# Reordering one iteration of a fused two-convolution kernel on TensorE, with small sums moved to another PSUM bank

## What is computed

```python
# stage 1, on g = groupnorm(x)
out = conv3x3(sign(tile(g, 4)), sign(w1), groups=4)           # 256 channels
out = relu(batchnorm(out))
out = conv3x3(sign(out), sign(w2), groups=4)
out = sum over the 4 groups of batchnorm(out) * lambda
x = x + relu(out + g)
# stage 2, on g = groupnorm(x)
mid = g * resized_mask                                         # one mask per image
att = sigmoid(conv7x7([mean_c(mid), max_c(mid), mask]))
out = mid * att
x = x + relu(5 * (instancenorm(out) * gamma + beta))
```

## Time and profile before

| | |
|---|---|
| median of 3 runs | 230.12 us (230.0 to 231.04) |
| profiled execution | 229.95 us, span of its instructions 228.1 us |
| granted TensorE clock, mean | 0.976 of full speed |
| TensorE matmul busy | 199.2 us (87%) |
| VectorE, ScalarE, GpSimd busy | 167.2 (73%), 174.7 (77%), 154.8 us (68%) |
| iteration 5 (no attention) | 9.94 us |
| iterations 13 and 14 | 23.25 us |
| from the loop's last turn to the end | 34.57 us |

### The profile page before, as it was taken

One profiled execution on the slowest core, in us unless ns is written; L12 is line 12 of the kernel. 1 busy time (PEld: TensorE's weight loads), 2 busy tenths in 40 slices (PEclk: granted clock), 3 DMA queues, 4 the chain that ended last, 5 costly groups with the idle time before them and its releaser, 6 DMA issues.

```text
span 228.1 us, 8994 instructions
## 1 busy us (share of the span) xinstructions
PE 199.2 (87%) x3807; PEld 124.3 (54%) x3807; DVE 167.2 (73%) x435; ACT 174.7 (77%) x230; POOL 154.8 (68%) x216
## 2 busy tenths in 40 slices
PE   8999996989799978998899989997999799898820
PEld 3556553646466546555665556565656466466810
DVE  2677264767766898967967899868576865988874
ACT  3697669888788886969888988989798978441293
POOL 8633552618161897779778979798959887846960
PEclk9999999999999999999999999999999999999955
DMA  6998005722218040834054405531352237134117
GB/s 212 317 282 316 11 5 162 196 90 65 82 39 234 20 141 7 256 102 138 9 164 122 136 12 149 142 80 68 117 170 65 83 80 210 42 105 145 71 70 282
DMA packets 12429, 28.48 MB, mean 125 GB/s; under 512 B 2293, under 2 KB 4213, under 8 KB 12389
## 3 DMA queue, kind: packets, MB, share of 16 engines
q1 hardware_dynamic: 11653, 26.84, 39.0%
q10 hardware_dynamic: 736, 1.06, 1.4%
HBM read 21.29 MB, written 6.61 MB: 122 GB/s over the span
## 4 chain that ended last, share of the span: by engine, by line
PE 30%; DVE 20%; POOL 19%; ACT 9%; DMA 8%; issue 8%; SPq 3%; POOLq 0%; DVEq 0%; ACTq 0%
DMA att_b<-attention_rows 8%; POOL o L416 7%; PE c L997 7%; POOL X L434 6%; PE c L1018 5%; DVE ve L769 5%; POOL o L429 4%; DVE bnst L737 4%; PE small L1079 4%; PE small L1087 3%; DVE red L816 3%; PE small L1067 3%; PE y L1042 2%; SPq L313 2%; PE c L1099 2%
## 5 line engine op out<-in xcount | busy, mean ns | idle before, releaser
L1018 PE MATMUL c<-S,w2t 64*32 64x392 f16 x2304 | 55.5, 331 | 1.2 <-issue 0.6
L997 PE MATMUL c<-E,w1t 64*128 64x420 f16 (+1 forms) x576 | 54.5, 330 | 0.7 <-ACT E L575 0.6
L797 DVE SCALAR_TENSOR_TENSOR RD<-RD,c 128x784 f16<-128x784 f16 x32 | 30.6, 956 | 27.2 <-ACT RD L603 27.2
L737 DVE BATCH_NORM_STATS2 bnst<-X 128x6 f32<-128x392 f32 x64 | 32.6, 552 | 17.0 <-POOL X L434 14.0
L1018 PEld LDWEIGHTS c<-S,w2t 64*32 64x32 f16 x2304 | 30.7, 92 | 20.6 <-issue 7.1
L997 PEld LDWEIGHTS c<-E,w1t 64*128 64x128 f16 x576 | 25.5, 94 | 22.5 <-issue 3.5
L1067 PE MATMUL small<-cs,o 128*112 128x130 f32 x196 | 28.7, 286 | 8.0 <-DVE red L818 7.5
L416 POOL TENSOR_TENSOR o<-o,mask_b 128x784 f32<-128x784 f32 x14 | 26.1, 1865 | 13.0 <-ACT o L625 13.0
L581 ACT ACTIVATE word<-c 128x840 int32<-128x840 f32 (+1 forms) x32 | 26.1, 815 | 9.5 <-PE c L997 9.3
L591 ACT ACTIVATE S<-word,thr_high 128x840 f16<-128x840 int16 (+1 forms) x32 | 30.6, 955 | 1.1
L1067 PEld LDWEIGHTS small<-cs,o 128*112 128x112 f32 x196 | 23.1, 176 | 13.7 <-DVE red L818 8.5
(11 more groups left out here) (134 smaller groups left out, 277.0 us busy)
## 6 DMA issues: line engine op xcount, KB each, us to landing
X<-in_x SPq DMA_DIRECT2D x16, 392.0 KB, 6.4
mask_b<-mask_rows SPq DMA_DIRECT2D x32, 196.0 KB, 3.4
out<-o SPq DMA_DIRECT2D x15, 392.0 KB, 3.8
att_b<-attention_rows SPq DMA_DIRECT2D x28, 196.0 KB, 4.9
o<-in_w ACTq DMA_DIRECT2D x1, 576.0 KB, 5.1
o<-in_masks SPq DMA_DIRECT2D x1, 512.0 KB, 7.0
band<-in_band SPq DMA_DIRECT2D x1, 441.0 KB, 9.2
cs<-in_cst SPq DMA_DIRECT2D x1, 434.0 KB, 4.7
```

The lines of the kernel that those rows point to most:

```text
L737: dve.bn_stats(bnst[:, n, t, i, :], src[:, HALF * i:HALF * (i + 1)]).then_inc(stats[n], 1)
L797: dve.scalar_tensor_tensor(RD[:, hh, 1, :], RD[:, hh, 0, :], -IMG / TINY, second_sums(t, hh), ALU.mult, ALU.add).then_inc(low2, 1)
L997: mm = pe.matmul(c1[:, 512 - n * (1 - i):512 + n * i], w1t[64 * i:64 * i + 64, s, :], window(START[i][hh], ROWS[hh], s, E[64 * i:64 * i + ...
L1018: mm = pe.matmul(second_bank(t, hh)[at:at + Q32, LOW + HALF * i:LOW + HALF * (i + 1)], w2t[64 * r:64 * r + 64, s, q, :], window(RH * half_ ...
```

## The change

TensorE's iteration now does both halves of conv1 of block k, the two first turns, and mix(k-1, 1), all ahead of conv2(k, 0); group_2 and the last turn follow conv2(k, 0), and attention directly the last turn. The group sums of blocks below 14 go to three columns of small[1] instead of y, in a layout with a third plane for veps (the variance plus epsilon), which VectorE writes to PSUM instead of SBUF. The batch variance is made by one scalar_tensor_tensor per block instead of a square and a sum per batch. mix no longer waits for var2; group_2 waits for the first turn's bank to be empty, terms2 for the last turn. VectorE does low_sums(k-1, 1) ahead of stats_x1(k-2), and finish_block(k-1) behind the first two reduce_chunks instead of last. ScalarE does the first word of a block ahead of relu_block, and high_sums(k-1, 1) ahead of the gates.

```diff
+        def group_at(t, m=2):
+            return small[1][:, AT_GROUP:AT_GROUP + m * t]
+        def group2_at(t, m=2):
+            return y[:, 0:m] if t >= POOL_X else small[1][:, AT_GROUP + 12:AT_GROUP + 12 + m]
...
             for k in range(1, NT):                 # ScalarE
+                words1(k, 0)
                 relu_block(k - 2)
-                words1(k, 0)
-                high_gates(k, 0)
-                low_gates(k, 0)
                 if k == 1:
                     keep_mask_h()
                 high_sums(k - 1, 1)
+                high_gates(k, 0)
+                low_gates(k, 0)
                 sign_x(k + 1)
...
             def group_terms(n, a, z, nm, ve, mean, chain, count, var):
-                ps = (group_at(z - a) if n == 0 else y[:, 0:2]).rearrange("p (t m) -> p m t", m=2)
+                ps = (group_at(z - a, 3) if n == 0 else group2_at(a, 3)).rearrange("p (m t) -> p m t", m=3)
                 dve.tensor_scalar(nm[:, a:z], ps[:, 0, :], -1.0, None, ALU.mult).then_inc(mean, 1)
-                dve.tensor_scalar(veps[:, n, a:z], ps[:, 1, :], EPS, None, ALU.add).then_inc(chain, 1)
+                dve.tensor_scalar(ps[:, 2, :], ps[:, 1, :], EPS, None, ALU.add).then_inc(chain, 1)
                 dve.tensor_tensor(dm[:, n, a:z], mv[:, n, a:z, 0], ps[:, 0, :], ALU.subtract).then_inc(chain, 1)
                 dve.wait_ge(chain, 2 * count)
-                if z - a == 1:
-                    dve.scalar_tensor_tensor(ve[:, a:z], dm[:, n, a:z], dm[:, n, a:z], veps[:, n, a:z],
-                                             ALU.mult, ALU.add).then_inc(var, 1)
-                    return
-                dve.tensor_tensor(dm2[:, a:z], dm[:, n, a:z], dm[:, n, a:z], ALU.mult).then_inc(square1, 1)
-                dve.wait_ge(square1, count - 3)
-                dve.tensor_tensor(ve[:, a:z], dm2[:, a:z], veps[:, n, a:z], ALU.add).then_inc(var, 1)
+                for t in range(a, z):
+                    last = dve.scalar_tensor_tensor(ve[:, t:t + 1], dm[:, n, t:t + 1], dm[:, n, t:t + 1],
+                                                    ps[:, 2, t - a:t - a + 1], ALU.mult, ALU.add)
+                last.then_inc(var, 1)
...
                     dve.wait_ge(group2, t + 1)     # terms2
+                    if 0 < t < POOL_X:
+                        dve.wait_ge(turned, turn_count(t - 1, 2))
...
+                low_sums(k - 1, 1)                 # VectorE's loop
                 stats_x1(k - 2)
-                low_sums(k - 1, 1)
                 reduce_chunks(k - 3, 0)
                 reduce_chunks(k - 3, 1)
+                finish_block(k - 1)
                 terms2(k - 2)
                 reduce_chunks(k - 3, 2)
                 low_sums(k, 0)
-                finish_block(k - 1)
...
                 pe.wait_ge(local[1], t + 1)        # group_2
-                wait(pe, y_added, t + 1 if t < NT - 2 else NT)
+                if t < POOL_X:
+                    pe.wait_ge(var1, 2 + sum(t + 2 >= k for k in TERMS_AT))
+                    if t > 0:
+                        pe.wait_ge(pooled, turn_count(t - 1, 0))
+                else:
+                    pe.wait_ge(y_added, NT)
...
                 if hh == 0:                        # mix
                     wait(pe, y_added, t)
-                elif t < NT - 1:
-                    wait(pe, var2, t)
-                else:
-                    pe.wait_ge(var2, NT - 2)
...
                 mix(k - 1, 0)                      # TensorE's loop
                 if k == 1:
                     resize_mask_w()
+                conv1(k, 1)
                 if k == 3:
                     pe.wait_ge(mask_rows, 2)
                 turn(k - 3, 0)
                 turn(k - 3, 1)
-                conv1(k, 1)
+                mix(k - 1, 1)
+                conv2(k, 0)
                 group_2(k - 2)
                 turn(k - 3, 2)
-                conv2(k, 0)
-                mix(k - 1, 1)
                 attention(k - 3)
```

More of the change, by code:

```diff
@@ L116, in build @@
         dm = sb("dm", [P, 2, NT], F32)
-        veps = sb("veps", [P, 2, NT], F32)
         nm1 = sb("nm1", [P, NT], F32)
@@ L121, in build @@
         nmr1 = sb("nmr1", [P, NT], F32)
-        dm2 = sb("dm2", [P, NT], F32)
         b1 = sb("b1", [P, NT], F32)
@@ L225, in inside @@
             return bass.AP(at.tensor, at.offset, [list(at.ap[0]), [PW, H], [1, W]])
-        def group_at(t):
-            return small[1][:, AT_GROUP:AT_GROUP + 2 * t]
+        def group_at(t, m=2):
+            return small[1][:, AT_GROUP:AT_GROUP + m * t]
+        def group2_at(t, m=2):
+            return y[:, 0:m] if t >= POOL_X else small[1][:, AT_GROUP + 12:AT_GROUP + 12 + m]
         x_in = [sem(f"x_in{t}") for t in range(NT)]
@@ L252, in build @@
         rstd1, rstd2, shift2 = sem("rstd1"), sem("rstd2"), sem("shift2")
-        bias1, shift1, square1 = sem("bias1"), sem("shift1"), sem("square1")
+        bias1, shift1 = sem("bias1"), sem("shift1")
         signed = sem("signed")
@@ L971, in group_1 @@
                     wait(pe, pooled, 3 * (next(k for k in TERMS_AT if TERMS_AT[k] == n) - 3))
-                pe.matmul(group_at(z - a), cs[:, K_PAIR:K_PAIR + P],
-                          mv[:, 0, a:z, :].rearrange("p t m -> p (t m)"), start=True, stop=True).then_inc(group1, 1)
+                pe.matmul(group_at(z - a).rearrange("p (m t) -> p m t", m=2), cs[:, K_PAIR:K_PAIR + P],
+                          mv[:, 0, a:z, :].rearrange("p t m -> p m t"), start=True, stop=True).then_inc(group1, 1)
             def group_2(t):
@@ L978, in group_2 @@
                 pe.wait_ge(local[1], t + 1)
-                wait(pe, y_added, t + 1 if t < NT - 2 else NT)
+                if t < POOL_X:
[4 more added lines that the diff above has]
+                    pe.wait_ge(y_added, NT)
                 if t == NT - 1:
                     pe.wait_ge(var2, t)
-                pe.matmul(y[:, 0:2], cs[:, K_PAIR:K_PAIR + P], mv[:, 1, t, :], start=True, stop=True)\
+                pe.matmul(group2_at(t), cs[:, K_PAIR:K_PAIR + P], mv[:, 1, t, :], start=True, stop=True)\
                   .then_inc(group2, 1)
```

## The result

The changed kernel takes 233.19 us (median, 233.06 to 233.75) against 230.12: ratio 1.0116, 95% interval 1.0082 to 1.015, so slower by more than this kernel's measurement is uncertain. Its profiled execution took 233.2 us with a span of 231.4, at a mean granted clock of 0.970. VectorE fell from 167.2 to 152.9 us busy, and the metric rose all the same.

What follows compares the result with a forecast made beforehand. TensorE was taken as the bound (87% busy), standing 15.0 us in the loop. -15.0 + 4.9 + 5.7 + 3.4 + 1.2 = +0.2 gave span 228.3, plus 1.85 around it and 0.17 for the median: 230.3 us; range 226.0 to 233.9.

Steps and rivals of the forecast that it cites:

- likeliest case: Whole kernel: the stalls change places and the time stays; chance 0.36, alone spanning 228.8 to 231.8 us.
- added waits: New TensorE stalls in the loop: +4.9 ahead of mix, +5.7 ahead of attention, +3.4 ahead of conv2(k, 1), in us.
- first term: TensorE's standing time in the block loop, all removed if nothing new is late: -15.0 us.
- point 4: Attention right behind the last turn waits for variance, last maximum and copy: 0.95 us six times, +5.7.
- point 5: ScalarE's relu behind the word delays high sums; conv2(k, 1) waits 0.85 us behind iterations 7, 9, 11, 13: +3.4.
- Point 3: mix(k-1, 1) waits for low_sums behind make_bias1 in iterations 2, 4, 7, 11, plus 0.45 at conv2(1, 1): +4.9 us.
- point 6: Iterations 5 and 6: no ScalarE-order stall, +0 beyond the wait ahead of attention.
- Points 1 and 2: Variance in PSUM falls to about 0.22 us; waits ahead of last turn and mix go, -15.0 if nothing new is late.
- Point 7: Tail: later group_2(13) makes block 13's turn 1.8 us later, finish_block(15) and last maximum about 1.2 later: +1.2.
- ScalarE did not catch up: Faster rival: ScalarE catches up, removing its conv2 stall and half the mix stall; 224.5 us at best, chance 0.30.
- GpSimd never waited for att_b: Slower rival: the attention load lands late and GpSimd waits for it; 232.3 to 234.3 us, chance 0.22.
- rival of VectorE's queue: Slower rival: low_sums(k, 0) stands behind the variance, conv2(k, 1) waits 0.3 us in ten iterations; 233.3 us, chance 0.08.

Runs made afterwards that it cites:

- e12: e7 plus, in even iterations from 6, the change's ScalarE order and low_sums(k-1, 1) ahead of stats_x1 on VectorE; 226.16 us, ratio to before 0.9819.
- e1: The kernel before with only the variance change (veps in PSUM, in a third plane of the group sums); 227.29 us, ratio to before 0.9883.
- e2: The after kernel, in its new order, with veps back in SBUF; 243.52 us, ratio to before 1.0591.
- e6: The after kernel with 13 idle matmuls ahead of the turns of block 13 in the tail; 233.62 us, ratio to before 1.0126.
- e3: The after kernel with ScalarE's relu_block put back ahead of the first word; 230.75 us, ratio to before 1.0018.
- e5: The after kernel with all of ScalarE's old order (relu, word, gates, high sums); 232.11 us, ratio to before 1.0035.
- e7: e1 with TensorE's last turn moved behind conv2(k, 0), ahead of mix(k-1, 1); 225.9 us, ratio to before 0.9778.

## Why the prediction came close, and where it was wrong

230.3 was forecast and 233.19 measured, inside the range. But the forecast was no change, and the change is slower by 1.2%. The mechanism was the likeliest case's, with the added waits of the loop and the tail mis-sized.

- **The first term, -15.0, stands.** It is what the loop took above the time of the same work without a wait. e12 shows that this time was right, 11.77 for an even iteration: its iteration 12 has no wait and takes 11.80, where the kernel before takes 13.31 with bracketed waits of 1.42:

```profile
145.59:157.39 11.80, 11.80 (x243) 7.56 (x240) 7.41 (x20) 10.73 (x14) 11.45 (x14) 1.00 0.26 75
```

- **The added waits were mis-sized: 15.8 against 14.0.** In the same measure the loop of the after kernel stands 15.8 (155.62 less the same work, 154.85 less 15.0), which gives the measured +0.77 where -1.0 was forecast. 14.3 of it are bracketed waits. The other 1.5 are overlap: a matmul behind a wait no longer overlaps the one ahead of it, about 0.08 us each time over the 18 waits. The busy column counts this as work, so length less busy time gives only 13.4 before and 14.3 after. The sum had this loss in point 4 alone (0.9 became 0.95).
- **The bracketed waits, point by point, came near the sum partly by luck.** Point 4 held (0.97 or 0.98 against 0.95 in 8 to 14, 1.02 and 1.13 in 4 and 6; 6.0 in all against 5.7), point 5 nearly (0.86, 0.65, 0.85, 0.65 against 0.85 each; 3.0 against 3.4). Point 3 was too high, 3.5 against 4.9: 0.75 and 0.74 against 1.0 in 7 and 11, 0.59 against 1.35 in 4; 0.98 against 1.1 in 2 and 0.40 against 0.45 at conv2(1, 1).
- **Missed: 1.8.** 1.06 in iteration 3, where group_1 writes to small[1] as attention does and waits for the same copy; and 0.20 and 0.53 in iteration 6, which point 6 put at nothing. These filled what point 3 had too much. Both of iteration 6 come from VectorE's queue: low_sums(5, 0) had its high sums at 74.43 but stood behind the variance, which waits for the last turn, and low_sums(5, 1) behind statistics that waited 1.60 for GpSimd. VectorE, end of iteration 5:

```profile
74.28 0.16 DVE L767 TENSOR_SCALAR nm<-small 128x1 f32<-128x1 f32 x1 [1.31 <-PE small L1070]
...
75.00 0.96 DVE L799 SCALAR_TENSOR_TENSOR RD<-RD,c 128x784 f16<-128x784 f16 x1
```

- **Points 1 and 2 held** in full: the variance is at 0.21 to 0.22 in the mean of all 32, and nothing waits for it ahead of the mix or the turn. e1 and e2 show both sides of it: -1.2% alone, +4.7% when it is taken out of the change.
- **Point 7 was mis-sized, +2.27 against +1.2.** Its own step was right to 0.1: the turn at T+15.23, forecast T+15.15, T+13.3 before. With the clock held, 1.7 of these 1.9 reach the attention (e6: T+19.23; before, 201.16 less 183.59 is T+17.57), not 1.2. The clock adds 0.8 there (T+20.05), and the spread gives 0.34 back: 3.79 at a granted clock of 0.99, against 4.13 at 0.90 in the trace before. How much of this belongs to the change stays open, since the spread's clock differs from kernel to kernel without a cause that these traces show.
- **Of the rivals** none decided the time. ScalarE did not catch up (e3, e5), GpSimd never waited for att_b in the after kernel, and of the waits that the rival of VectorE's queue describes there is one, the 0.20 of iteration 6.

What stays open: what sets the tail's clock behind the turns and in the spread (3.79 to 5.36 us over these kernels with the same 32 matmuls), and whether e7 can be freed of its waits of 0.54 with GpSimd's chain as it is; in e12 it was late sooner.

## What to carry to other kernels

A removed wait is worth what its place shows only while no other wait moves into it: list for each reordered call which producer is now last, and keep independent matmuls between the one that a producer waits for and its consumer; here the place of one mix, with one call on VectorE, was worth 2%. Count what a wait costs by the length of the stretch with and without it: it is longer than the bracket of the wait, and the busy column hides the difference. When a change bundles a cheap local repair with a reordering, time the repair alone first: here it brought -1.2%, and the whole change +1.2%.

## What the runs showed of the hardware

Behind a standstill of TensorE of about 2 us the granted clock was mostly low, and not always: 0.65 behind 2.23 us (after), 0.54 behind 1.80 (e2), where four of five attentions ran long (2.25 to 3.36 us) and one, behind 2.01, at its full 1.91. In the traces of all fourteen kernels, from iteration 2 to the spread, 22 standstills took 1.72 to 2.97 us; in the 5 us behind them 17 had a lower clock and 5 had 1.00 throughout. Behind those of 1.0 to 1.54 us it stayed at 1.00. The same wait of 1.73 us in iteration 2 left it at 1.00 in the kernel before and not in e1 (0.62) and e12. So two profiled executions can differ by a microsecond in a stretch whose instructions and waits are the same. In e2 the loop's waits grew by 4.6 us, and TensorE's busy time in it by another 5.1.

The same 32 matmuls of the spread took 3.79 us at a granted clock of 0.99 (after) and 5.32 at 0.69 (e12).

A VectorE instruction of one element per partition, running beside a GpSimd multiply, took 1.26 us (e2) with both of its tensors in SBUF, and 0.22 (after) once one was in PSUM; its pointer scalar (the operand with one value per partition) lay in SBUF in both.

A wait of TensorE cost about 0.06 to 0.1 us more than its bracket: 1.54 against 1.42 for the two of iteration 12 before (13.31 less 11.77).
